# The last stage of an eight-expert layer with plain stores only, and the residual x added on chip

## What is computed

```python
x = x + _layernorm(attention(_layernorm(x)))          # called x1 here
x = x + _layernorm(experts(_layernorm(x)))            # the change is in this line's last step
# _layernorm(v) = (v - mean(v)) / sqrt(var(v) + 1e-05), over the 256 floats of a token
```

## Time and profile before

| | us |
|---|---|
| three executions | 1088.45, 1094.52, 1095.66 |
| the profiled execution | 1096.26 |
| its span, first to last instruction | 1093.8 |
| last store issued by SP, from the span's start | 1090.92 |
| TensorE, VectorE, ScalarE, GpSimd busy | 980.5, 696.7, 713.2, 430.4 |

### The profile page before, as it was taken

How to read it: one execution, slowest core, us unless ns; L and a number is a source line. 1 busy time by engine, 2 the same in 40 slices (tenths; PEclk the granted TensorE clock), 3 DMA queues, 4 the chain that set the end, 5 groups by cost and what they waited for, 6 DMA issues and landing times.

```text
span 1093.8 us, 16766 instructions
## 1 busy us (share of the span) xinstructions
PE 980.5 (90%) x5468; PEld 663.2 (61%) x5468; DVE 696.7 (64%) x1883; ACT 713.2 (65%) x1090; POOL 430.4 (39%) x357
## 2 busy tenths in 40 slices
PE   5699999999999999969879997999999999989950
PEld 3223544545354454524578886888888888878850
DVE  5154376573946656364696689566766776768847
ACT  2587867766776776646746664577666777667835
POOL 5121030332314132223343446745555445445435
PEclk8799999999999999989989999999999999999985
DMA  7655625528073584842413442765665645567739
GB/s 269 140 156 151 237 55 169 177 71 275 16 241 89 161 293 152 275 158 73 169 37 109 118 121 59 232 188 146 151 160 132 168 129 122 124 177 214 205 45 291
DMA packets 57694, 171.10 MB, mean 156 GB/s; under 512 B 10384, under 2 KB 26896, under 8 KB 51728
## 3 DMA queue, kind: packets, MB, share of 16 engines
q1 hardware_dynamic: 38698, 137.99, 38.3%
q0 software_dynamic: 18768, 31.76, 15.0%
q10 hardware_dynamic: 150, 0.41, 0.2%
HBM read 98.55 MB, written 71.57 MB: 156 GB/s over the span
## 4 chain that ended last, share of the span: by engine, by line
PE 61%; DVE 20%; ACT 6%; issue 6%; POOL 4%; DMA 3%; DVEq 0%; ACTq 0%; POOLq 0%; SPq 0%
PE PH L1747 14%; PE PO L971 6%; PE PS L988 6%; PE PB L1051 6%; PE PY L1777 5%; PE PB L1777 4%; ACT E L595 3%; PE PA L1038 3%; PE PY L1782 3%; PE PY L1778 3%; DVE ST L200 2%; PE PB L1778 2%; DVE HP L1688 2%; DVE ON L742 2%; PE PB L1112 1%
## 5 line engine op out<-in xcount | busy, mean ns | idle before, releaser
L595 ACT ACTIVATE E<-PS,VV 128x1024 f32<-128x1024 f32 x256 | 270.6, 1118 | 73.1 <-PE PS L988 70.2
L1747 PE MATMUL PH<-XP,W1P 128*128 128x512 f32 (+1 forms) x1104 | 232.7, 369 | 15.1 <-DVE HP L1688 12.1
L1747 PEld LDWEIGHTS PH<-XP,W1P 128*128 128x128 f32 x1104 | 185.3, 192 | 55.7 <-DVE HP L1688 16.3
L1517 POOL DMA_INDIRECT choice_rows<-Y,DI x78 | 126.9, 1627 | 114.4 <-DVE Y L1648 83.7
L988 PE MATMUL PS<-OPB,OPA 102*128 102x512 bf16 x512 | 140.7, 390 | 14.5 <-DMA OPA<-norm_parts 7.9
L1688 DVE TENSOR_TENSOR HP<-PH,HP 128x512 fp32r<-128x512 f32 x156 | 106.7, 686 | 64.3 <-ACT HP L1597 63.7
L1592 ACT ACTIVATE PH<-PH,B 128x512 f32<-128x512 f32 (+1 forms) x184 | 107.5, 596 | 57.7 <-PE PH L1747 48.5
L971 PE MATMUL PO<-E,VA 128*32 128x512 f32 x1024 | 143.8, 611 | 0.0
L988 PEld LDWEIGHTS PS<-OPB,OPA 102*128 102x128 bf16 x512 | 37.4, 98 | 161.2 <-ACT E L595 75.9
L473 POOL DMA_INDIRECT expert_rows<-PAY,SLOT x64 | 62.7, 979 | 158.0 <-issue 81.4
L1583 ACT CAST W2P<-WG 128x512 fp32r<-128x512 f32 x92 | 56.8, 621 | 104.3 <-PE PB L1778 63.1
(11 more groups left out here) (245 smaller groups left out, 1554.5 us busy)
## 6 DMA issues: line engine op xcount, KB each, us to landing
expert_rows<-ZERO SPq DMA_DIRECT2D x8, 4160.0 KB, 13.0
WG<-experts SPq DMA_DIRECT2D x23, 1152.0 KB, 5.6
WG<-experts SPq DMA_DIRECT2D x23, 1028.0 KB, 5.6
OPB<-q_parts SPq DMA_DIRECT2D x192, 64.0 KB
q_parts<-QP SPq DMA_DIRECT2D x48, 128.0 KB
OPA<-q_parts SPq DMA_DIRECT2D x31, 192.0 KB
choice_rows<-ZERO SPq DMA_DIRECT2D x1, 5120.0 KB, 14.3
X<-x SPq DMA_DIRECT2D x8, 512.0 KB, 7.4
```

What stands on the lines that cost most here:

```text
L595: a.activation(E[:, s % 2, h, :, :], PS[:, u % 2, :, :], ACT.Exp, scale=vec("tau_t")[:, 4 * (s // 2) + h:4 * (s // 2) + h + 1]).then_inc(e ...
L1517: g.indirect_dma_start(out=ys, out_offset=IND(ap=DI[:, t % 3, i:i + 1], axis=0), in_=Y[:, t % 2, i, :], in_offset=None, compute_op=ALU.add ...
L1747: last = m.matmul(PH[:, u % BANKS, at:at + w], W1P[:, a, k * HID + c * P:k * HID + c * P + P], XP[:, o, k, 0:w], start=(k == 0 and (a, o) ...
```

## The change

The early plain stores of x in stage 2 and the accumulating stores in stage 3 are both gone. All nine chunks are stored plainly by SP, in order, each after its own semaphore added[i]. X is added on chip for all nine: GpSimd adds chunks 0, 2 and 4 (BY_POOL), in the place where it issued an accumulating store before, and DVE adds chunks 1, 3, 5 and 6 in the loop, each two chunks behind its statistics as before, and 7 and 8 after it. The loads, the statistics, the power and the product, and ScalarE's list are untouched.

```diff
@@ -29,7 +29,6 @@
 LEFT = SUBTILES - 2 * BEGUN
 BLOCKS = HALVES * SUBTILES
 DUMPS = 8
-KEPT = 5
 STEPS_E = TOK // SUB
 VE = 2 * NE
 ROW = D + 4
...
@@ -1478,10 +1476,6 @@
                 sp.wait_ge(b2_ready, t)
                 sp.wait_ge(w2_lo, PIECES * t)
             sp.dma_start(WG2[:, :], experts2[bass.ds(row, P), :]).then_inc(w2_loaded, 16)
-            if BEGUN <= t < BEGUN + KEPT:
-                b = t - BEGUN
-                sp.wait_ge(begun["x1_added"], b + 1)
-                sp.dma_start(out[b * N:(b + 1) * N].rearrange("(p c) e -> p c e", c=C), X[:, C * b:C * b + C, :]).then_inc(begun["x_kept"], 16)
 
     def gpsimd(pool, do):
         g = nc.gpsimd
...
@@ -1810,12 +1804,12 @@
     return y_sent, y_rows, Experts(sync, gpsimd, scalar, vector, tensor)
 
 
-def stage3(nc, made, X, half, ys, out, y_sent, y_rows, x_kept):
+def stage3(nc, made, X, half, ys, out, y_sent, y_rows):
 
     f32 = mybir.dt.float32
     ACT, ALU = mybir.ActivationFunctionType, mybir.AluOpType
     CHUNKS = [(b, 0, C) for b in range(B - 1)] + [(B - 1, c, C // 2) for c in (0, C // 2)]
-    BY_STORE = KEPT
+    BY_POOL = (0, 2, 4)
     LAG = 2
     sb, pb, sem = made
     YC = sb("YC", [P, B, C, D], f32)
...
@@ -1825,7 +1819,7 @@
     R = sb("RF", [P, 4, B, C], f32)
     loaded = [sem(f"y_loaded{b}") for b in range(B)]
     var_ready, scaled, normed, roots = sem("var_ready"), sem("scaled"), sem("normed"), sem("roots")
-    added, stored, out_added, links = sem("added"), sem("stored"), sem("out_added"), sem("finish_links")
+    added, stored, links = [sem(f"added{i}") for i in range(len(CHUNKS))], sem("stored"), sem("finish_links")
     yv = ys[0:TOK].rearrange("(b p c) e -> b p c e", p=P, c=C)
     ov = out.rearrange("(b p c) e -> b p c e", p=P, c=C)
 
...
@@ -1838,26 +1832,27 @@
             sp.wait_ge(y_sent[r], y_rows[r])
         for b in range(B):
             sp.dma_start(YC[:, b, :, :], yv[b]).then_inc(loaded[b], 16)
-        for i in range(BY_STORE, len(CHUNKS)):
-            b, c, n = CHUNKS[i]
-            sp.wait_ge(added, i - BY_STORE + 1)
+        for i, (b, c, n) in enumerate(CHUNKS):
+            sp.wait_ge(added[i], 1)
             sp.dma_start(ov[b][:, c:c + n, :], T[:, b, c:c + n, :]).then_inc(stored, 16)
-        sp.wait_ge(stored, 16 * (len(CHUNKS) - BY_STORE))
-        sp.wait_ge(out_added, 16 * BY_STORE)
+        sp.wait_ge(stored, 16 * len(CHUNKS))
+
+    def add(eng, i):
+        b, c, n = CHUNKS[i]
+        eng.tensor_tensor(T[:, b, c:c + n, :], T[:, b, c:c + n, :], X[:, C * b + c:C * b + c + n, :], ALU.add
+                          ).then_inc(added[i], 1)
 
     def gpsimd(pool):
         g = nc.gpsimd
-        pool.wait_ge(x_kept, 16 * BY_STORE)
         for i, (b, c, n) in enumerate(CHUNKS):
             var, nmean, r, bias = (R[:, q, b, c:c + n] for q in range(4))
             pool.wait_ge(var_ready, 2 * i + 2)
             g.tensor_tensor(r, var, half[:, 0:n], ALU.pow).then_inc(roots, 1)
             pool.wait_ge(roots, i + 1)
             g.tensor_tensor(bias, nmean, r, ALU.mult).then_inc(scaled, 1)
-            if 1 <= i <= BY_STORE:
-                of, at, rows = CHUNKS[i - 1]
+            if i - 1 in BY_POOL:
                 pool.wait_ge(normed, done(i))
-                g.dma_start(ov[of][:, at:at + rows, :], T[:, of, at:at + rows, :], accum_op=ALU.add).then_inc(out_added, 16)
+                add(g, i - 1)
 
     def vector(dve):
         v = nc.vector
...
@@ -1866,12 +1861,6 @@
         def link(i):
             at[0] += 1
             i.then_inc(links, 1)
-
-        def add(i):
-            b, c, n = CHUNKS[i]
-            dve.wait_ge(normed, done(i + 1))
-            v.tensor_tensor(T[:, b, c:c + n, :], T[:, b, c:c + n, :], X[:, C * b + c:C * b + c + n, :], ALU.add
-                            ).then_inc(added, 1)
 
         for i, (b, c, n) in enumerate(CHUNKS):
             dve.wait_ge(loaded[b], 16)
...
@@ -1883,10 +1872,12 @@
             dve.wait_ge(links, at[0])
             v.tensor_scalar_add(R[:, 0, b, c:c + n], MV[:, b, c:c + n, 1], EPS).then_inc(var_ready, 1)
             v.tensor_scalar_mul(R[:, 1, b, c:c + n], MV[:, b, c:c + n, 0], -1.0).then_inc(var_ready, 1)
-            if i - LAG >= BY_STORE:
-                add(i - LAG)
+            if i >= LAG and i - LAG not in BY_POOL:
+                dve.wait_ge(normed, done(i - LAG + 1))
+                add(v, i - LAG)
         for i in range(len(CHUNKS) - LAG, len(CHUNKS)):
-            add(i)
+            dve.wait_ge(normed, done(i + 1))
+            add(v, i)
 
     def scalar(act):
         for i, (b, c, n) in enumerate(CHUNKS):
```

More of the change, by code:

```diff
@@ L301, in program @@
         rows_clear, x1_ready, x1_links, choices_clear = sem("rows_clear"), sem("x1_ready"), sem("x1_links"), sem("choices_clear")
-        x_kept = sem("x_kept")
         half_ready = sem("half_ready")
@@ L1153, in program @@
         begun = dict(begun_ready=begun_ready, pre_full=pre_full, pre_free=pre_free, q_stored=q_stored, n_stored=n_stored, s_full=s_full,
-                     rows_clear=rows_clear, choices_clear=choices_clear, x1_added=x1_added, x_kept=x_kept, pv_done=pv_done, po_read=po_read, late_free=late_free)
+                     rows_clear=rows_clear, choices_clear=choices_clear, pv_done=pv_done, po_read=po_read, late_free=late_free)
         apart = ExitStack()
@@ L1157, in program @@
             inner = ExitStack()
-            y_sent, y_rows, experts = stage2(nc, make(inner), tables, tables_ready, const, rows, ys, experts1, experts2, begun, PB, X, out)
+            y_sent, y_rows, experts = stage2(nc, make(inner), tables, tables_ready, const, rows, ys, experts1, experts2, begun, PB)
             inner.close()
-            last = stage3(nc, make(apart), X, HALF[:, :, :].rearrange("p a c -> p (a c)"), ys, out, y_sent, y_rows, x_kept)
+            last = stage3(nc, make(apart), X, HALF[:, :, :].rearrange("p a c -> p (a c)"), ys, out, y_sent, y_rows)
             block = apart.enter_context(nc.Block())
@@ L1378, with stage2 @@
 Experts = collections.namedtuple("Experts", "sync gpsimd scalar vector tensor")
-def stage2(nc, made, tables, tables_ready, const, rows, ys, experts1, experts2, begun, PB, X, out):
+def stage2(nc, made, tables, tables_ready, const, rows, ys, experts1, experts2, begun, PB):
     f32, f32r, i32 = mybir.dt.float32, mybir.dt.float32r, mybir.dt.int32
```

## The result

Over seven executions each, the changed kernel took 1099.11 us at the median (1094.77 to 1101.21) and the kernel before 1094.52. The ratio is 1.0051, with a 95% interval of 1.003 to 1.0072: some 5.6 us longer by the ratio. I had forecast 1096.9, 2.4 us longer, within 1%. The direction and the range held; the loss is twice what my sum gave.

What follows compares the result with a forecast made beforehand. TensorE was taken to bound most of the kernel, GpSimd to pace the last stage. A last stage 2.7 us longer, less 0.3 gained in stage 2, gave +2.4 us: 1096.9 us, range 1089 to 1102.

Steps and rivals of the forecast that it cites:

- the range: Whole kernel: predicted time between 1089 us, where stage 2 pays in full, and 1102 us, the end of the held-port case.
- my sum: Whole kernel: last stage 2.7 us longer, stage 2 gains 0.3, together +2.4 us, a median of 1096.9.
- the ring of waits: Last stage: DVE statistics, GpSimd power and product, then ACT; GpSimd sets the pace at some 2.3 us per chunk.

## What to carry to other kernels

Moving elementwise work to an engine with idle time is worth what the ring of waits makes of it: three adds of 2.35 us on GpSimd cost 4.75 of the stage, the same three on VectorE 27.10 - 23.89 = 3.2. The kernel before had the better answer still, an accumulating store whose issue takes GpSimd 0.9 us. Before placing a wide GpSimd operation, list every VectorE operation that will run beside it, the tiny ones too, and search the trace for each form's longest duration beside GpSimd, not for its mean. Where cutting one delay moves nothing, look for a second ring of the same length before dropping the theory.

## What the runs showed of the hardware

- A VectorE tensor-scalar operation of 128x4 floats (0.17 us) is held until a running GpSimd add ends (2.22 us). Aggregations are not: in the run with the adds one turn later, four of them took their usual 0.38 from 1085.60 on, inside the add of 1085.58.
- The hold is by instruction: with the add in four pieces of 0.72 it was 0.60 at most in that run, and 0.69 in the one with the pieces one turn later.
- A power on GpSimd does not hold a VectorE add that begins inside it (one case in the last stage, 1072.95 in the run with pieces), but is itself held by one that began before it: 1.91 us for 1.02, ending 0.9 us after the add, and 1.60 for 0.70 on half a chunk, ending 0.55 after it.
- GpSimd's add of two full streams of 1024 floats takes 2.35 us, and 0.72 for 256 floats; with one operand repeated, 1024 take 1.89.
- A plain store of 512 KB lands 2.4 to 2.6 us after its issue with little else under way, an accumulating one 5.7 to 6.5.
